# A pairwise-interaction tower on one core: diagonals in the tiling of the fills, blocks formed behind sums, the last layer on two column groups

## The reference

```python
viW = jnp.einsum('bpd,pde->bpe', vi, W)      # vi = e[:, i], vj = e[:, j]
z   = jnp.einsum('bpe,bpe->bp', viW, vj)
h = concatenate([z, dense_ctx], axis=1)      # 780 + 16 columns
h = maximum(h @ W_top1 + b_top1, 0)          # 512
h = maximum(h @ W_top2 + b_top2, 0)          # 256
y = h @ W_top3                               # 1
```

## Time and profile before

| | us |
|---|---|
| median of 3 runs | 353.68 (353.11 to 353.86) |
| profiled execution | 353.03 |
| its span, first to last instruction | 351.1 |
| TensorE busy | 344.3 (98%) |
| VectorE busy | 256.7 (73%) |
| GpSimd busy | 227.4 (65%) |
| ScalarE busy | 70.3 (20%) |

### The profile page before, as it was taken

One profiled execution on the slowest core, in us unless ns is written; L12 is line 12 of the kernel. 1 busy time (PEld: TensorE's weight loads), 2 busy tenths in 40 slices (PEclk: granted clock), 3 DMA queues, 4 the chain that ended last, 5 costly groups with the idle time before them and its releaser, 6 DMA issues.

```text
span 351.1 us, 4306 instructions
## 1 busy us (share of the span) xinstructions
PE 344.3 (98%) x1682; PEld 115.1 (33%) x1682; DVE 256.7 (73%) x246; ACT 70.3 (20%) x112; POOL 227.4 (65%) x176
## 2 busy tenths in 40 slices
PE   7999999999999999999999999999999999999997
PEld 3222333233332333333333333333233333334342
DVE  3965877786878787789889987898998989970010
ACT  1243703333213030303040302103021030000011
POOL 5665466566466466368895879888889999970000
DMA  7646231221212221822112220212110000000000
GB/s 213 231 148 199 79 111 49 82 80 23 80 31 71 80 78 39 329 84 71 56 32 69 75 75 16 69 66 78 60 67 10 0 2 0 0 2 0 0 0 0
DMA packets 10740, 24.18 MB, mean 69 GB/s; under 512 B 3537, under 2 KB 4305, under 8 KB 10594
## 3 DMA queue, kind: packets, MB, share of 16 engines
q1 hardware_dynamic: 6482, 19.72, 16.0%
q0 software_dynamic: 4096, 4.20, 4.9%
q10 hardware_dynamic: 144, 0.00, 0.0%
HBM read 23.91 MB, written 0.00 MB: 68 GB/s over the span
## 4 chain that ended last, share of the span: by engine, by line
PE 97%; ACT 1%; DVE 1%; issue 0%
PE u L440 52%; PE zp L461 20%; PE xp L415 8%; PE u L471 7%; PE xp L402 3%; PE u L428 2%; PE u L507 2%; PE u L479 2%; ACT xq L373 1%; ACT xt L368 1%; DVE prod L552 0%; PE xp L512 0%; PE xp L514 0%; DVE prod L554 0%; DVE prod L541 0%
## 5 line engine op out<-in xcount | busy, mean ns | idle before, releaser
L552 DVE TENSOR_TENSOR prod<-u,xq 128x1024 f32<-128x1024 f32 x180 | 206.8, 1214 | 44.4 <-PE u L440 39.9
L440 PE MATMUL u<-xt,w_ring 64*128 64x512 f32 x760 | 189.9, 619 | 1.6 <-ACT xt L368 1.3
L331 POOL DMA_INDIRECT gath<-in_tbl,ids_sb x128 | 124.2, 970 | 75.8 <-DMA gath<-in_tbl,ids_sb 42.3
L339 POOL TENSOR_TENSOR prod<-prod 128x1024 f32<-128x1024 f32 x44 | 102.9, 2367 | 10.0 <-DVE prod L552 9.7
L440 PEld LDWEIGHTS u<-xt,w_ring 64*128 64x128 f32 x760 | 63.9, 185 | 117.9 <-DVE prod L552 63.4
L461 PE MATMUL zp<-prod,sel_sb 128*32 128x512 f32 x604 | 72.5, 597 | 0.0
L368 ACT ACTIVATE xt<-xp 128x512 f32<-128x512 f32 x20 | 12.0, 598 | 197.8 <-PE xp L402 153.9
L373 ACT ACTIVATE xq<-xt 32x512 f32<-32x512 f32 x80 | 50.2, 627 | 2.1
L461 PEld LDWEIGHTS zp<-prod,sel_sb 128*32 128x32 f32 x604 | 17.5, 109 | 51.1 <-issue 46.3
L530 DVE TENSOR_SCALAR xq<-late,row_sb 128x1024 f32<-128x1024 int32 x32 | 22.0, 746 | 11.6 <-PE xp L415 6.9
L415 PE MATMUL xp<-xq,late 128*64 128x512 f32 x128 | 28.3, 595 | 0.7 <-ACT xt L368 0.7
(11 more groups left out here) (22 smaller groups left out, 39.0 us busy)
## 6 DMA issues: line engine op xcount, KB each, us to landing
w_ring<-in_w_cell SPq DMA_DIRECT2D x24, 512.0 KB
late<-in_ids_small SPq DMA_DIRECT2D x4, 512.0 KB, 5.2
gath<-in_tbl,ids_sb POOLq DMA_INDIRECT x128
late<-in_w_top SPq DMA_DIRECT2D x1, 1792.0 KB
late<-in_small SPq DMA_DIRECT2D x3, 512.0 KB
late<-in_small SPq DMA_DIRECT2D x2, 256.0 KB
late<-in_w_top SPq DMA_DIRECT2D x1, 512.0 KB
wd_sb<-in_w_diag SPq DMA_DIRECT2D x1, 320.0 KB
```

The source lines that it names most:

```text
L331: pool.indirect_dma_start(gath[:, g % GR, t, half, :], None, tables[f], bass.IndirectOffsetOnAxis(ap=ids_sb[:, t, f:f + 1], axis=0),).then ...
L339: pool.tensor_tensor(prod[:, lo % PR, :, :], prod[:, lo % PR, :, :], prod[:, hi % PR, :, :], ALU.add).then_inc(folded, 1)
L440: mm = pe.matmul(u[:, n % UR, a, :], w_ring[rows, q % RW, at * P:(at + 1) * P], xt[rows, moving % XR, :], start=True, stop=True)
L552: dve.tensor_tensor(prod[:, n % PR, :, :], u[:, n % UR, :, :], x, ALU.mult).then_inc(prod_ready, 1)
```

## The change

Three edits. First, the diagonals' weights are padded with zeros to 128 columns, so that their fills use the same two tiles of 64 x 128 as all others and write the whole buffer; VectorE reads the same halves of it as before. The load of these weights is twice as large. Second, `item_slot` puts an item from the 8th on into the last slot that directly follows a slot with sums, among those that its bounds allow. This gives the slots 29, 35, 43, 57, 65, 79, 90, 106, 124, 136, 154 and 176. Third, the last layer's matmuls are split into two halves of 256 rows of the batch, on column groups 0 and 1, with results in two PSUM banks; ScalarE copies one and VectorE the other, and each is stored by its own transfer.

```diff
@@ -174,9 +174,13 @@
 
 def item_slot(k):
 
+
     if k < 2:
         return 0
-    return max(FIRST_SLOT[k] - (1 if k < 4 else 2), FIRST_SLOT[k - 1])
+    at = max(FIRST_SLOT[k] - (1 if k < 4 else 2), FIRST_SLOT[k - 1])
+    if k < 8:
+        return at
+    return max([n + 1 for n in SUM_SLOT if FIRST_SLOT[k - 1] <= n + 1 <= at], default=at)
 
 
 def look_up_slot(k):
@@ -205,7 +209,7 @@
         xq = sb("xq", [P, NQ, 2, B])
         row_sb = sb("row_sb", [P, TC])
         w_ring = sb("w_ring", [P, RW, PIECE * P])
-        wd_sb = sb("wd_sb", [P, NB // 2, D])
+        wd_sb = sb("wd_sb", [P, NB // 2, P])
         prod = sb("prod", [P, PR, 2, B])
         ident_sb = sb("ident_sb", [P, P])
         sel_sb = sb("sel_sb", [P, 62])
@@ -225,7 +229,7 @@
 
         h1_sb = prod[:, 0:2, :, :].rearrange("p a c n -> p (a c) n")
         h2_sb = prod[:, 2, :, :]
-        y_sb = prod[0:1, 3, 0, :]
+        y_sb = [prod[32 * c:32 * c + 1, 3, 0, 0:B // 2] for c in range(2)]
 
         zeros = prod[:, PR - 1, :, :]
 
@@ -233,7 +237,8 @@
         xp = psum("xp", [P, B])
         zp = psum("zp", [P, B])
         h1_ps = [u[:, (NS - 3 + m // 2) % UR, m % 2, :] for m in range(M1)]
-        h2_ps, y_ps = u[:, (NS - 1) % UR, :, :], xp[0:1, :]
+        h2_ps = u[:, (NS - 1) % UR, :, :]
+        y_ps = [xp[0:1, 0:B // 2], zp[32:33, 0:B // 2]]
 
         warm_ready = sem("warm_ready")
         ids_in = sem("ids_in")
@@ -311,9 +316,10 @@
                     sp.dma_start(b1_sb[:, :], b1).then_inc(tower_in, 16)
                     sp.dma_start(b2_sb[:, :], b2).then_inc(tower_in, 16)
                     sp.dma_start(z_sb[P - DENSE:P, NZ - 1, :], dense).then_inc(tower_in, 16)
-            sp.wait_ge(y_ready, 1)
-            sp.dma_start(out, y_sb).then_inc(stored, 16)
-            sp.wait_ge(stored, 16)
+            sp.wait_ge(y_ready, 2)
+            for c in range(2):
+                sp.dma_start(out[:, c * B // 2:(c + 1) * B // 2], y_sb[c]).then_inc(stored, 16)
+            sp.wait_ge(stored, 32)
 
         @block.gpsimd
         def _(pool):
@@ -386,7 +392,7 @@
             act.activation(h2_sb[:, 0, :], h2_ps[:, 0, :], ACT.Relu,
                            bias=b2_sb[:, 0:1]).then_inc(h2_act, 1)
             act.wait_ge(y_mm, 1)
-            act.activation(y_sb, y_ps, ACT.Copy).then_inc(y_ready, 1)
+            act.activation(y_sb[0], y_ps[0], ACT.Copy).then_inc(y_ready, 1)
 
         @block.tensor
         def _(pe):
@@ -425,8 +431,8 @@
                 if what == "diag":
                     pe.wait_ge(diag_in, 16)
                     pe.wait_ge(x_ready, k + 1)
-                    pe.matmul(u[D:P, n % UR, 0, :], wd_sb[0:D, m, :], xt[0:D, (k - 1) % XR, :], start=True, stop=True)
-                    pe.matmul(u[0:D, n % UR, 1, :], wd_sb[D:P, m, :], xt[D:P, k % XR, :],
+                    pe.matmul(u[:, n % UR, 0, :], wd_sb[0:D, m, :], xt[0:D, (k - 1) % XR, :], start=True, stop=True)
+                    pe.matmul(u[:, n % UR, 1, :], wd_sb[D:P, m, :], xt[D:P, k % XR, :],
                               start=True, stop=True).then_inc(u_filled, 1)
                     return
                 q, at = divmod(W_AT[n], PIECE)
@@ -508,10 +514,14 @@
                                    start=t == 0, stop=t == M1 - 1)
                     if t == M1 - 1:
                         mm.then_inc(h2_mm, 1)
+
             pe.wait_ge(h2_act, 1)
-            pe.matmul(y_ps, w3_sb[:, 0:1], h2_sb[:, 0, :], start=True, stop=False)
+            for c in range(2):
+                pe.matmul(y_ps[c], w3_sb[:, 0:1], h2_sb[:, 0, c * B // 2:(c + 1) * B // 2], start=True, stop=False)
             pe.wait_ge(h2_dve, 1)
-            pe.matmul(y_ps, w3_sb[:, 1:2], h2_sb[:, 1, :], start=False, stop=True).then_inc(y_mm, 1)
+            for c in range(2):
+                mm = pe.matmul(y_ps[c], w3_sb[:, 1:2], h2_sb[:, 1, c * B // 2:(c + 1) * B // 2], start=False, stop=True)
+            mm.then_inc(y_mm, 1)
 
         @block.vector
         def _(dve):
@@ -566,6 +576,8 @@
             dve.wait_ge(h2_mm, 2)
             dve.tensor_scalar(h2_sb[:, 1, :], h2_ps[:, 1, :], b2_sb[:, 1:2], 0.0,
                               ALU.add, ALU.max).then_inc(h2_dve, 1)
+            dve.wait_ge(y_mm, 1)
+            dve.tensor_copy(y_sb[1], y_ps[1]).then_inc(y_ready, 1)
 
 
 def pair_number(order, i, j):
@@ -595,10 +607,11 @@
 
 
 def diag_weights(w, order):
-    got = np.zeros((P, NB // 2, D), w.dtype)
+
+    got = np.zeros((P, NB // 2, P), w.dtype)
     for m in range(NB // 2):
-        got[:D, m] = pair_weight(w, order, 4 * m, 4 * m + 1)
-        got[D:, m] = pair_weight(w, order, 4 * m + 3, 4 * m + 2)
+        got[:D, m, D:] = pair_weight(w, order, 4 * m, 4 * m + 1)
+        got[D:, m, :D] = pair_weight(w, order, 4 * m + 3, 4 * m + 2)
     return got
```

## The result

| | before | after |
|---|---|---|
| median, us | 353.73 (353.11 to 353.86) | 356.66 (355.94 to 357.27) |
| profiled execution, us | 353.03 | 356.43 |
| its span, us | 351.1 | 354.3 |
| ratio of the times | | 1.0087, interval 1.0069 to 1.0105 |

The change makes the kernel 2.9 us slower by the medians (2.4 to 3.7 by the interval of the ratio); 356.9 was forecast, with 355.5 to 358.4.

The account below looks back on a forecast made before the run. VectorE was taken to pace the main stretch, a relay over three PSUM buffers. 353.03 + 4.1 - 0.35 - 0.23 = 356.55, or 357.2 from the runs' median; 356.9 us was forecast between them, range 355.5 to 358.4.

Parts of the forecast that it names:

- Moved forms, +4.1: Main stretch: twelve forms directly behind sums lengthen VectorE's standstills by 7.0 us, less 2.9 won back.
- what comes back: Turns of the main stretch: what the forms' old places and the diagonals had cost there is gone, 2.9 us.
- The first rival: Whole kernel: TensorE is the bound throughout, so all edits gain, -5.2 us, 348.2; chance 0.07.
- The second: Main stretch: 0.585 is paid twelve times and the 2.9 is not won, +6.4 us, 359.8; chance 0.04.
- the third: Forms behind sums: a switch hidden behind the sum makes a form cost 0.44, +1.6 us, 355.1; chance 0.05.
- the fourth: Earlier forms or small tables: a gather or table lands late, +6.8 us, 360.3; chance 0.02.
- the last: Main stretch: VectorE makes up the standstills from idle time, so -0.6 us, 352.8; chance 0.02.
- Diagonals, -0.35: Padded diagonals: only slot 7's, in the opening, saves time, 0.35 us; bounds -0.35 to 0.
- The 0.9 given to the diagonals of the main stretch: Main stretch: what seven padded diagonals would save alone, without the moved forms, 0.9 us.
- Last layer, -0.23: End: halved matmul -0.43, two copies -0.15, second store +0.35; sum -0.23 us, between -0.4 and +0.6.
- The 96 waits: Main stretch: weight loads idled 96 times, 63.4 us together, for VectorE's products, taken as evidence that VectorE paces.

Follow-up runs that it names:

- four_forms: Kernel before with only items 8, 11, 16 and 19 formed directly behind sums; 355.18 us, +0.9 against before.
- forms_only: Kernel before with only the forms of items 8 to 19 moved directly behind sums; 358.38 us, +4.4 against before.
- narrow_after: Changed kernel with VectorE's products and GpSimd's folds over half the batch's rows; 343.31 us, against 346.62 for the kernel before halved alike.
- last_layer_only: Kernel before with only the last layer split on two column groups, two copies and two stores; 353.49 us, -0.5 against before.
- no_forms: Changed kernel with the old item_slot: padded diagonals and split last layer, forms not moved; 352.43 us, -1.5 against before.
- after_again: The changed kernel measured once more, nothing altered; 357.62 us, +3.7 against before.
- single_sums: late_places with one batch per group of sums in place of two, and some forms at new slots; 347.17 us, -6.8 against before.
- diag_only: Kernel before with only the diagonals padded to 128 columns and their larger load; 352.49 us, -1.5 against before.
- late_places: Changed kernel with forms late in a turn, where TensorE waits for VectorE, or at their old places; 351.98 us, -2.3 against before.

## Why the prediction was right

**Moved forms, +4.1.** From the fill of slot 22 to that of slot 199 the changed kernel's trace is 4.11 us longer. Both terms are seen apart: each form behind a sum adds 0.585 (2.47 to 3.05, four_forms' 3.06), and what comes back is seen in turns (11.93 to 11.62) and in the vanished 0.42. Turn by turn there is nothing else: ten of the twelve turns closed by a form grow by 0.58 to 0.59; the two that also lose form 8 or form 11 grow by 0.07 and 0.08; six others shrink, two by 0.32, two by 0.39 and two by 0.24; the rest, from slot 22 on, stay within 0.01. The first rival (TensorE the bound throughout) falls with forms_only; narrow_after shows what its world would be. The second (nothing comes back) falls with the same turns, the third with the 0.59 of the form itself, the fourth because TensorE met no late gather in the changed kernel, the last because VectorE made nothing up.

**Diagonals, -0.35.** The opening gave 0.34 (the fill of slot 10 comes 0.27 earlier, the first one 0.07 later). Around slot 17's diagonal came 0.41 more, between the fills of slots 16 and 22, and I had put it at nothing. The reason is not the fill saved: VectorE's idle before the product of slot 16 was 0.83 before and is 0.42 now.

```profile
63.03 1.23 DVE L552 TENSOR_TENSOR prod<-u,xt 128x1024 f32<-128x1024 f32 x1 [0.83 <-PE u L440]
```

```profile
62.36 1.23 DVE L562 TENSOR_TENSOR prod<-u,xt 128x1024 f32<-128x1024 f32 x1 [0.42 <-ACT xt L374]
```

From the fill of slot 16 to that of slot 20 the four kernels with the old diagonals that I read (before, forms_only, last_layer_only, four_forms) took 4.23 to 4.42 us, and five with padded ones 3.89 to 4.07. So it goes with the diagonals, but the same order of slots at 30 and 31 shows no such thing in the kernel before, and what holds the product is open. It starts 0.38 to 0.57 after its fill's end in the four and 0.05 to 0.22 in the five. It is the second product behind a sum, as in the stalls above, and may be one of them; that was not shown. With the opening's 0.34 the term is -0.75, outside the -0.35 to 0 that it was given. The 0.9 given to the diagonals of the main stretch without the moved forms holds: in no_forms' turns it is 2 x 0.32 + 0.14 + 0.15 = 0.93.

**Last layer, -0.23.** From the start of the last weight load the changed kernel saves 0.42 to the copies and 0.16 to the first store, and pays 0.31 for the second issue: -0.27.

**The sum.** The span grows by 3.2 where the sum said 3.5, the 0.41 around slot 17 being the larger part of the difference. By the medians the time grows by 2.9, and by 3.7 in after_again. That the 356.9 lies within 0.3 of the measured 356.66 is in part luck: it was set on a start between the profiled 353.03 and the median 353.68, and from the median alone the same sum gives 357.2. Two rivals' times are 0.1 off their own terms (355.0 and 360.2), which changes nothing.

**The 96 waits.** One ground of the prediction was weaker than it looked. In single_sums, from 94 to 118 us, weight loads wait for products 7 times, 3.9 us together, and lengthen no fill; in the kernel before, from 91 to 114.5, it is 6 times and 3.8. So the list of waits doesn't say which engine paces. The paced form of the fill and the length of the turn do.

## What to carry to other kernels

Where two engines hand on through a few buffers, neither a chain that names one of them for 97% of the span nor a list of waits tells which of them paces: look for the paced form of the same instruction (here 1.13 against 0.86) and for what the other engine does in the long pauses. Work that is not part of the relay belongs where the first engine waits for the second, early enough before the next pause that the lead is won back; put directly behind a pause it cost its full length here, 0.585, even though it saved work. And a pause longer than the buffers cover may be better split: here two of 1.85 in place of one of 3.57 brought eight fills and their sums from 11.61 to 10.98 us.

## What the runs showed of the hardware

VectorE's second product behind a standstill was sometimes late with its fill long there: by 0.81, 0.21 and 0.21 of added or lengthened idle in forms_only's trace, 0.69 in after_again's, none at these places in the first trace of the changed kernel. In diag_only's trace (slot 65) and in late_places' (slots 29, 51, 65 and 90) it was the first product: it started 0.6 to 1.2 us after its fill's end, where 0.05 is usual. Each cost its turn between 0.5 and 1.2 us. The traces of before, last_layer_only and four_forms have none of this size. Single runs of the kernel before differed by up to 4.5 us in one session (352.99 to 357.46), which such stalls may be a part of; that was not shown. Around slot 36 ScalarE, GpSimd and a load of weights are at work in the traces with the stall (forms_only, after_again) and in that without it (the changed kernel); no experiment here separates them, so its cause is open.
